# Attention stage written out tile by tile: rows turned before they are scaled, router logits out of the projections

## What is computed

```
def attention(x, Wq, bq, Wk, bk, Wv, bv, Wg, bg, Wo, bo):       # x is rmsnorm(input, norm1_scale)
    q = phi(apply_rope(heads(x @ Wq + bq)))                      # 16 heads of 16
    k = phi(apply_rope(heads(x @ Wk + bk)))                      # phi = elu + 1
    v = heads(x @ Wv + bv)
    g = heads(sigmoid(x @ Wg + bg))
    # chunks of 64 rows, in order, one state (S, Z) for each sequence and head
    S = S + einsum('bhtd,bhte->bhde', kc, vc);  Z = Z + kc.sum(axis=2)
    out = gc * (einsum('bhtd,bhde->bhte', qc, S) / (einsum('bhtd,bhd->bht', qc, Z) + 1e-6))
    return out @ Wo + bo

x = x + attention(...)
xn = rmsnorm(x, norm2_scale)
logits = xn @ router_W + router_b                                # 8 experts, two for each row
x = x + (gelu MoE of xn, capacity 1280 rows an expert)
x = layernorm(input + x);  x = layernorm(x + (silu-gated MoE of 8 experts on layernorm(x)))
```

## Time and profile before

| | |
|---|---|
| median of 3 runs | 1633.08 us (1632.31 to 1634.97) |
| the profiled execution | 1631.68 us, of which span 1629.9 us |
| PE busy | 1520.2 us (93%) |
| PEld busy | 1451.8 us (89%) |
| DVE busy | 1046.6 us (64%) |
| ACT busy | 736.8 us (45%) |
| POOL busy | 786.6 us (48%) |
| mean granted TensorE clock | 0.956 |

### The profile page before, as it was taken

One profiled execution on the slowest core, in us unless ns is written; L12 is line 12 of the kernel. 1 busy time (PEld: TensorE's weight loads), 2 busy tenths in 40 slices (PEclk: granted clock), 3 DMA queues, 4 the chain that ended last, 5 costly groups with the idle time before them and its releaser, 6 DMA issues. The chain is left out here.

```text
span 1629.9 us, 37588 instructions
## 1 busy us (share of the span) xinstructions
PE 1520.2 (93%) x11761; PEld 1451.8 (89%) x11761; DVE 1046.6 (64%) x2953; ACT 736.8 (45%) x1698; POOL 786.6 (48%) x795
## 2 busy tenths in 40 slices
PE   6999996699999999999967999999999999999990
PEld 4777774699999999999866999999999999999990
DVE  5888886676766676676465655565565665565553
ACT  3555552454545455555344434434343434343324
POOL 3778884156656665665241334334334434434420
PEclk9999997599999999999985999999999999999995
DMA  7011010223433433342332132313213231411216
GB/s 245 33 35 35 32 36 33 93 44 93 98 62 78 99 92 50 91 126 42 89 138 94 33 104 33 107 29 86 56 26 107 36 103 27 113 30 27 34 19 212
DMA packets 63715, 119.07 MB, mean 73 GB/s; under 512 B 14384, under 2 KB 52784, under 8 KB 61488
## 3 DMA queue, kind: packets, MB, share of 16 engines
q0 software_dynamic: 35840, 42.38, 16.0%
q1 hardware_dynamic: 27824, 76.07, 12.8%
HBM read 79.71 MB, written 38.71 MB: 73 GB/s over the span
## 5 line engine op out<-in xcount | busy, mean ns | idle before, releaser
L855 POOL DMA_INDIRECT acc<-E_ysb,IDX x160 | 258.2, 1614 | 135.5 <-ACT E_ysb L945 66.3
L982 DVE TENSOR_TENSOR E_hraw<-E_sg,bank 128x256 f32<-128x256 f32 x320 | 134.6, 421 | 286.1 <-ACT E_sg L918 286.1
L850 POOL DMA_INDIRECT E_mg<-meta,IDX x160 | 150.9, 943 | 337.1 <-DVE E_gate L966 311.2
L1035 PE MATMUL bank<-E_xT,ws 128*128 128x256 f32 x960 | 272.4, 284 | 5.0 <-DVE E_xT L957 5.0
L1036 PE MATMUL bank<-E_xT,ws 128*128 128x256 f32 x960 | 271.9, 283 | 0.0
L1037 PE MATMUL bank<-E_xT,ws 128*128 128x256 f32 x960 | 271.7, 283 | 0.0
L993 DVE TENSOR_TENSOR E_hT<-E_hraw,E_hT 128x256 fp32r<-128x256 f32 x640 | 259.5, 416 | 0.0
L989 DVE CAST E_hT<-E_hraw 128x256 fp32r<-128x256 f32 x640 | 203.2, 318 | 58.5 <-ACT E_hraw L921 51.6
L918 ACT ACTIVATE E_sg<-bank 128x256 f32<-128x256 f32 x320 | 121.6, 384 | 256.4 <-PE bank L1037 254.6
L1035 PEld LDWEIGHTS bank<-E_xT,ws 128*128 128x128 f32 x960 | 183.2, 191 | 6.0 <-issue 5.8
L1035 PE MATMUL bank<-ws,E_hT 128*128 128x256 f32 x640 | 183.8, 287 | 0.0
(11 more groups left out here) (195 smaller groups left out, 4045.8 us busy)
## 6 DMA issues: line engine op xcount, KB each, us to landing
wraw<-in_w_ffn SPq DMA_DIRECT2D x8, 3072.0 KB, 10.5
wraw<-in_w_moe SPq DMA_DIRECT2D x8, 2048.0 KB, 8.0
X<-acc SPq DMA_DIRECT2D x16, 512.0 KB, 6.9
X<-in_x SPq DMA_DIRECT2D x8, 512.0 KB, 9.3
xn<-A_xn SPq DMA_DIRECT2D x32, 128.0 KB, 1.7
acc<-X SPq DMA_DIRECT2D x32, 128.0 KB, 1.7
acc<-X SPq DMA_DIRECT2D x8, 512.0 KB, 2.9
out<-C_xo SPq DMA_DIRECT2D x8, 512.0 KB, 2.8
```

Source lines behind the costliest of these rows:

```text
L850: nc.gpsimd.indirect_dma_start(out=mg[:, j, :], out_offset=None, in_=meta_dram, in_offset=at_slots(u, j)).then_inc(s_gm, 16)
L855: nc.gpsimd.indirect_dma_start(out=acc_dram, out_offset=at_slots(u, j), in_=ysb[:, j, :], in_offset=None, compute_op=ALU.add).then_inc(s_y ...
L982: V.tensor_tensor(hraw[:, f % RING, :], sg[:, f % RING, :], bank[f % RING][:, UW:2 * UW], ALU.mult).then_inc(s_hm, 1)
L1035: nc.tensor.matmul(out, wh, mh, start=first, stop=False)
```

## The change

The change rewrites `attention_phase`. All 37 steps are written out for every engine, and the loop, its register values and the marks that the queues set in it (`passed`) go. Tiles now run in their order, first sequence 0 and then sequence 1, with one PSUM bank for the state, which is cleared when a sequence starts.

- The raw rows are turned. The row factor r1 is applied where the projections leave PSUM, as a scalar operand for each partition of a multiply-add.
- The router's weights (times the second norm's scale) stand behind the 1024 columns of the projections: x @ Wr comes with the gate's columns. Wo @ Wr and bo @ Wr are computed once, in TensorE's step 0, so that the output product yields its part of the logits in 8 more columns. The logits of x1 are then scaled by r2 into `LG`, from which routing reads them. The turning of xn and its product go.
- phi is max(y + 1, min(exp(y), 1)): DVE adds 1 with the sum of the rotation, ACT takes exp(y), DVE does both minimum and maximum.
- The gate times 1/den is one factor (POOL), and DVE multiplies the numerators in PSUM by it.
- ACT makes the gate's affine step. v and gate have projections and banks of their own. The weights of the first expert are split in 16 pieces of 256 columns, in steps 6 to 21.
- Two more small loads come ahead of the wait for the early loads; the first load of rows is half as large.

The diff, cut:

```diff
-def run_tiles(eng, step, before_loop, in_loop=None):
-    for t in range(-LEAD, LOOP_FROM):
-        step(lambda d: fixed_tile(t + d))
-    before_loop()
-    with eng.Fori(0, LOOP_STEPS) as j:
...
+def run_tiles(eng, step):
+    for t in range(-LEAD, NT + LAG):
+        step(t, lambda d, t=t: t + d if 0 <= t + d < NT else None)
```

POOL, in the order of its new queue (left out between X and r2: rb, its two halves as before; behind xb: r1 and the expert's weights):

```diff
+                if (n := at(-1)) is not None:
+                    pool.wait_ge(s_rden, n + 1)
+                    pool.wait_ge(s_g, n + 1)
...
+                    nc.gpsimd.tensor_tensor(by_head(gr[:, n % 2, :]), by_head(gt[:, n % 2, :]),
+                                            rden[:, :, :].rearrange("p k h -> p (k h)").unsqueeze(2).to_broadcast([P, H, DK]),
+                                            ALU.mult).then_inc(s_gr, 1)
+                if (n := at(-2)) is not None:
+                    nc.gpsimd.tensor_tensor(X[:, n, :], X[:, n, :], x1[:, n % 2, 0:D], ALU.add).then_inc(s_xacc, 1)
+                if (n := at(1)) is not None:
...

+                if (n := at(-2)) is not None:
+                    nc.gpsimd.tensor_tensor(r2[:, n:n + 1], ssq2[:, n:n + 1], mhalf[:, :], ALU.pow).then_inc(s_r2, 1)
+                if (n := at(-1)) is not None:
+                    nc.gpsimd.tensor_tensor(xb[:, n % 2, 0:D], X[:, n, :], bo[:, :], ALU.add).then_inc(s_xb, 1)
+                    nc.gpsimd.tensor_tensor(xb[:, n % 2, D:DX], lx[:, n % 2, :], bor[:, :], ALU.add).then_inc(s_xbx, 1)
```

DVE (left out: den and rden ahead of x1; behind the first mask the low half of xT, ra, the second mask, and rot, which now adds 1):

```diff
+            def step(t, at):
+                if (n := at(-1)) is not None:
...

+                if (n := at(-2)) is not None:
+                    dve.wait_ge(s_wo, n + 1)
...
+                    V.tensor_tensor(x1[:, n % 2, :], wo_ps, xb[:, n % 2, :], ALU.add).then_inc(s_x1, 1)
+                if (n := at(0)) is not None:
+                    dve.wait_ge(s_ex, n + 1)
...
+                    V.scalar_tensor_tensor(out=phi[:, n % 2, :], in0=ex[:, n % 2, :], scalar=1.0, in1=rot[:, n % 2, :],
+                                           op0=ALU.min, op1=ALU.max).then_inc(s_phi, 1)
+                    dve.wait_ge(s_pjv, n + 1)
+                    V.scalar_tensor_tensor(out=va[:, n % 2, :, 0:P], in0=b_pv[:, 0:D].rearrange("p (k c) -> p k c", k=KD),
+                                           scalar=r1[:, n:n + 1], in1=bqkvg[:, 2 * D:3 * D].rearrange("p (k c) -> p k c", k=KD),
+                                           op0=ALU.mult, op1=ALU.add).then_inc(s_va, 1)
+                    dve.wait_ge(s_pjg, n + 1)
+                    V.scalar_tensor_tensor(out=gt[:, n % 2, :], in0=b_pg[:, 0:D], scalar=r1[:, n:n + 1], in1=bqkvg[:, 3 * D:4 * D],
+                                           op0=ALU.mult, op1=ALU.add).then_inc(s_gt, 1)
+                if (n := at(1)) is not None:
+                    V.scalar_tensor_tensor(out=qk[:, :], in0=b_p0[:, :], scalar=r1[:, n:n + 1], in1=bqkvg[:, 0:2 * D],
+                                           op0=ALU.mult, op1=ALU.add).then_inc(s_qk, 1)
+                if (n := at(-1)) is not None:
+                    dve.wait_ge(s_gr, n + 1)
+                    V.tensor_tensor(og[:, n % 2, :].rearrange("p (k c) -> p k c", k=KD), num_ps[:, :, 0:P],
+                                    gr[:, n % 2, :].rearrange("p (k c) -> p k c", k=KD), ALU.mult).then_inc(s_og, 1)
+                if (n := at(0)) is not None:
+                    mask(n, 0)
...

```

PE, whose step is now: q/k of at(1), raw rows of at(2), phi and chunk 0 of at(0), v of at(1), chunk 1, og of at(-1), gate and router of at(1), numerators of at(0), output product of at(-1). Left out of `extend_weights`: 4 products with woT and 2 with bob, 8 columns each:

```diff
+            def project(n, out, cols):
+                for k in range(KD):
+                    for m, (a, b) in enumerate(((0, 0), (0, 1), (1, 0))):
+                        ins = nc.tensor.matmul(out, xT[:, n % 2, a, k, :], wsp[:, b, k, cols],
...
+            def extend_weights():
+                pe.wait_ge(loads, 16 * 5)
+                for m in range(KD):
+                    for k in range(KD):
+                        ins = nc.tensor.transpose(b_to[:, m * D + k * P:m * D + (k + 1) * P], wo[:, k, m * P:(m + 1) * P], ident)
+                ins.then_inc(s_wt, 1)
+                pe.wait_ge(s_wte, 1)
...

+            def step(t, at):
+                if t == 0:
+                    extend_weights()
...
+                    project(n, b_p0[:, :], slice(0, 2 * D)).then_inc(s_pj0, 1)
+                        ins = nc.tensor.transpose(tx_ps[:, k, :], X[:, n, k * P:(k + 1) * P], ident)
+                    project(n, b_pv[:, 0:D], slice(2 * D, 3 * D)).then_inc(s_pjv, 1)
+                    project(n, b_pg[:, 0:DX], slice(3 * D, WX)).then_inc(s_pjg, 1)
```

More of the change, by code:

```diff
@@ L102, with attention_phase @@
 LAG = 2
[L103 to L116, removed]
-def run_tiles(eng, step, before_loop, in_loop=None):
-    for t in range(-LEAD, LOOP_FROM):
-        step(lambda d: fixed_tile(t + d))
-    before_loop()
-    with eng.Fori(0, LOOP_STEPS) as j:
[L125 to L133, removed]
+WX = 4 * D + E
+DX = D + E
+W_STEPS = range(6, 22)
+WCHUNK = 4 * HID // len(W_STEPS)
+def run_tiles(eng, step):
+    for t in range(-LEAD, NT + LAG):
+        step(t, lambda d, t=t: t + d if 0 <= t + d < NT else None)
+def attention_phase(nc, bank, io, X, LGA, cst, small, wraw, ws0):
     used = []
@@ L183, in attention_phase @@
-        s_ssq1, s_r1, s_xs, s_tx, s_xT, s_xl = map(sem, ("ssq1", "r1", "xs", "tx", "xT", "xl"))
-        s_pj0, s_pj1, s_qk, s_ra, s_rb, s_rot, s_vg = map(sem, ("pj0", "pj1", "qk", "ra", "rb", "rot", "vg"))
-        s_mn, s_ex, s_phi, s_th, s_g = map(sem, ("mn", "ex", "phi", "th", "g"))
+        early, loads, xg = sem("early"), sem("loads"), [sem(f"xg{g}") for g in range(5)]
+        s_w, s_wh, s_wl, s_cst, s_wt, s_wte, s_wx, s_wxe = map(sem, ("w", "wh", "wl", "cst", "wt", "wte", "wx", "wxe"))
@@ L207, in halves, with by_head, loaded @@
         def halves(ap):
             return ap.rearrange("p (h a d) -> p h a d", a=2, d=HALF)
+        def by_head(ap):
+            return ap.rearrange("p (h d) -> p h d", d=DK)
+        def loaded(eng, n):
+            for g, span in enumerate(spans):
+                if span.start == n:
+                    eng.wait_ge(xg[g], 16)
         block = ctx.enter_context(nc.Block())
@@ L465, in _, with mask @@
-            run_tiles(dve, step, lambda: None)
+                V.tensor_tensor(wsp[:, 1, k, :], wqkvg[:, k, :], wsp[:, 0, k, :].bitcast(F32), ALU.subtract).then_inc(s_wl, 1)
+            dve.wait_ge(loads, 16 * 5)
+            for m in range(KD):
+                V.tensor_scalar(bob[:, m, :], ident, 0.0, bcol[:, m:m + 1], ALU.mult, ALU.add).then_inc(s_w, 1)
+            dve.wait_ge(s_cst, 4)
+            def mask(n, c):
+                after(dve, s_num, n)
+                dve.wait_ge(s_sa, 2 * n + c + 1)
+                V.tensor_tensor(sm[:, c, :, :], s_ps, hmask, ALU.mult).then_inc(s_mk, 1)
@@ L467, in _, with add_chunk @@
+            run_tiles(dve, step)
         @block.tensor
         def _(pe):
-            pe.wait_ge(early, 16 * 3)
-            pe.wait_ge(s_cst, 3)
-            for b in range(BATCH):
-                nc.tensor.matmul(b_s[b][:, 0:KD * SW], zeros[:, 0:P], zeros[:, :], start=True, stop=True)
-            def add_chunk(t, c):
+            pe.wait_ge(early, 16 * 5)
+            pe.wait_ge(s_cst, 4)
+            def add_chunk(n, c):
                 rows = slice(c * CHUNK, (c + 1) * CHUNK)
+                if n % TPB == 0 and c == 0:
+                    nc.tensor.matmul(b_s[:, 0:KD * SW], zeros[:, 0:P], zeros[:, :], start=True, stop=True)
```

512 lines of the change are left out of this document (227 added, 285 removed).

## The result

The changed kernel takes 1607.8 us (median of 4 runs, 1606.5 to 1615.1) against 1633.9 for before: ratio 0.985, 95% interval 0.983 to 0.987. That is 26.1 us by the medians and 24.6 between the two profiled executions. I had forecast 1619, with 1611 to 1629. The direction is right, the forecast gain of 14.2 us is little more than half of the measured one, and the time lies outside the range.

A forecast was written before the change was run, and what follows sets the result against it. TensorE was taken to bound the attention stage without waits. 29 steps x (7.70 - 7.25) = -13.0, start +0.6 and end -1.8 gave -14.2 us: 1633.1 to 1619, range 1611 to 1629.

The forecast's parts named there:

- TensorE's part of a step: Attention steps: TensorE's groups, summed without the router product and xn transposes, take 7.12 us in place of 7.70.
- What bounds the kernel now: TensorE: Attention stage: TensorE's matmul groups follow one another without a visible wait, 7.70 us a step.
- The wait that may take its place: Second chunk: TensorE waits for mask 0 from VectorE's chain, about 0.13 a step, making 7.25 us.
- The stall of 0.13: Ahead of the second chunk: TensorE there at +3.52, mask ending at +3.56 plus 0.1 for the semaphore.
- The range's lower end: Whole kernel: 1611 us, with the start at its lower bound and no stall.
- What lies beside it: Other engines in a step: VectorE moves away from the limit; idle time on POOL and ScalarE hides their new work.
- Start: Step 0: small products and Wo transposes delay phi's transposes by 2.7, less savings; net +0.6 us, bounds -1 and +3.
- End: Output product of tile 30 to routing: 10.7 in place of 13.3, then +0.8 for later x1 and phi; -1.8 us.
- Written out: The attention loop: writing it out gains nothing, since straight steps take 7.72 us, as long as the loop's.
- The sign on the later stages: Stages behind 262 us: the prediction counts as wrong if they move by over 2 us.
- The fixed price of narrow matmuls: Narrow projections: 0.156 a matmul, 0.46 more a step, 7.7 us; total 1632, no change; chance 0.05.
- The two-pass multiply-add: VectorE's va, gate, qk from PSUM: 1.5 more a step, stall 1.65, step 8.8, total 1663; chance 0.05.

The follow-up runs named there:

- e8: Kernel before, with TensorE transposing og twice into the same place, adding 0.2 us of work between second chunk and numerators; one run, 1635.9 us.
- e3: Changed kernel, with the gate and router projection moved from ahead of the numerators to behind the output product; 1617.4 us.
- e1: Kernel before, with the second half of the v/gate projection moved from behind the output product to ahead of the numerators; ratio to before 1.000.
- e9: Kernel before, loop written out, half projection ahead of the numerators, POOL's piece of expert weights moved behind the second norm's power; 1624.8 us, ratio 0.995.
- e4: Changed kernel, with the router's former TensorE work (two transposes, an 8-column product) put back as dead work in every step; 1623.8 us.
- e10: Changed kernel, with the products of Wo and bo in TensorE's step 1 and POOL's piece of weights behind the next step's X + x1; 1604.8 us.
- e6: Changed kernel, with POOL's X + x1 moved from ahead of the rotation to behind the second norm's power; 1625.6 us.
- e2: Kernel before, with its 24 looped steps written out and nothing else; ratio to before 0.999.
- e5: Changed kernel, with the products of Wo and bo with the router's weights moved from TensorE's step 0 to step 1; median 1607.9 us.

## Why the prediction was right in its direction and wrong in its size

- **TensorE's part of a step.** This is the step that failed: 7.12 us forecast, 6.84 measured. The output product (0.80), chunks, transposes of raw rows and phi were as said. The narrow groups were 0.90 each for 0.84 and 0.86, the q/k projection 1.58 for 1.49, 0.2 more together, and og and the numerators 0.46 less. The miss is in two numbers copied from the earlier trace rows as work: "transposes of og 0.37, numerators 0.91". They measure 0.19 and 0.63 in the new order. Of the 0.28 on the numerators at least 0.22 was a wait for mask 1, which I had ruled out with "none is a wait that I can see" (e8 filled it for free; e3 brought it back). The 0.18 on og's transposes goes with the neighbours, a product of full width in place of the 64-column numerators, and is no gain: in e1 and e9, where both figures fall although the work is the same, the output product grows by 0.19, and in the changed kernel the q/k projection is 0.20 longer than in e3. The projection in between was in the diff; I had costed its width and not what it does for the wait behind it.
- **"What bounds the kernel now: TensorE".** Not quite so. e9 shows at most 7.41 us of TensorE's work in a step of before; 0.26 was waiting, for the mask, and in every second step, when that is taken away, for xn. So 7.67 to 6.86 falls into 0.26 for the order of the queues and 0.55 for the rest, which is what the earlier trace rows price the router's work at; e4 gives 0.51 to 0.62 for it. My rows priced the second part rightly, and the first is what I had put at nothing.
- **The wait that may take its place.** The chain on VectorE came out at +3.12 because two errors cancel: 0.05 to 0.06 on each pointer operation and their neighbours, and a shorter way from the output product to x1 (0.39, not 0.57). The stall of 0.13 is not there, since the q/k and the narrow projection ahead of it are longer than I said (TensorE is there at 3.66, not at 3.52). The range's lower end assumed no stall and nothing more, so it could not hold a hidden wait.
- **What lies beside it.** POOL's queue hides its work, as said, but not for free: in the 16 steps with a piece of weights the piece runs into phi, which grows to between 0.80 and 0.87 (1.04 in one of them), and these steps take 0.1 more, about 1.8 us in all. e10 takes that back. The changed kernel is near a second limit: e6 moved one POOL operation of 0.7 to 1.2 us and lost 17.8 us.
- **Start.** +0.6 forecast, +3.4 measured. The block ahead of the phi transposes stands where I had put it, behind the copy (which ends at 22.70), but three terms were off. The exp ahead of it ends 0.97 earlier than before and not 1.93; from there to the transposes it is 4.29 us and not 3.5, with products of 1.36 instead of 1.08 and part of 20 to 30 us at 1.2 GHz; and the clearing of the state had no term at all, though the change names it. It costs 1.04 us here and 0.65 at 137.54, where the second sequence starts. In e10, where the clock held, tile 2's projection starts at 28.92 with the products moved.
- **End.** -1.8 forecast, -3.3 + 1.1 = -2.2 measured. The last output product took 1.16 and not 2.07 us: TensorE was at 1.2 GHz in before there (0.50 in 269 to 272 us), and at full clock in the changed kernel, where the low stretch (0.51 in 243.4 to 246.8) hit the product ahead of it, which took 1.85 for 1.13.
- **Written out.** Nothing, as forecast: e2, 0.999. The rule of the Trainium skill weighed there (Runtime: NRT & Kernel Launch, "Instruction fetch mechanics") has no visible price in this kernel; it speaks of a branch target outside the two pages held, and no run here shows whether this loop's was.
- **The sign on the later stages.** I had called myself wrong if the stages behind routing moved by over 2 us. They moved by 3.6, and by up to 5.8 between kernels that do not differ there: the sign was set inside the scatter.
- **Rivals.** The fixed price of narrow matmuls did not come: twelve of them cost 1.80 us with all changes of shape, 0.05 more than the six wide ones. So the figures of the Trainium skill's page TensorE: Matmul & The Clock Gate ("Back-to-back issue gap") do not carry over to fp32r products with a weight load each; 0.118 us a matmul at 256 columns and 0.233 to 0.248 at 512 do. The two-pass multiply-add did not come either.

## What to carry to other kernels

A group of matmuls that takes longer than its like elsewhere may contain a wait, even when no idle time is marked: compare the starts of its members, or add dummy work in front and see if the step grows. A longer time alone proves nothing: og's transposes took 0.37 and 0.19 without a wait, and the difference turned up in a neighbour. When one wait is taken away and the time stays, read the trace once more before you conclude that it was none; the next queue may have been within 0.3 us of it. In a queue written out by hand, put an operation that nobody waits for where the engine waits anyway, and cost each step of a moved group by what stands behind it, not only by its width. When two engines slow each other, look which of the two began first before you name the partner.

## What the runs showed of the hardware

- What a TensorE group takes, from start to start, depends on the group behind it: og's transposes take 0.37 ahead of the 64-column numerators (before, e2, e3) and 0.19 ahead of a full-width product (changed kernel, e1, e4, e9, e10). The output product takes 0.78 ahead of a projection and 0.97 ahead of the router's 8 columns (e1, e9), a q/k projection 1.58 behind the output product and 1.38 behind another projection (e3). The orders compared have equally many changes of the array's shape, so no run here gives the price of one.
- In the start of the program (20 to 50 us) the granted clock sometimes falls back to 1.2 GHz: windows of 10 us have 0.83, 0.66, 0.71 and even 0.50 in different runs, 1.00 in others. In the changed kernel TensorE had been idle for 2.54 us, up to 22.75, before it fell; in e5 for 1.18 us, up to 22.33, and then the clock stayed low although TensorE was busy for all of 30 to 40 us. After 0.97 of idle time before kept its clock and e2 did not. In e5 the fall is worth about 8 us (a projection at 44.2, in e10 at 35.7), and it goes with the difference between that kernel's runs at 1605 (mean clock 0.958) and at 1615 (0.950). What decides it these runs don't show.
- When a VectorE operation with two SBUF inputs and a POOL operation overlap, the one that began later is stretched. Phi takes 0.68 with `X + x1` starting behind it (0.46 of overlap, and `X + x1` grows from 0.73 to 1.05), and 0.85, 1.04, 1.11 and 1.23 where a POOL operation that began first still runs for 0.30, 0.50, 0.56 and 0.68 of it (changed kernel and e6). The Trainium skill says that the two share their SBUF interfaces (GPSIMD Engine Reference, section "1. Specifications"), contending where VectorE has two SBUF inputs; the trace agrees. Operations of VectorE from PSUM (0.41, 0.43) did not grow.
